# Batch 0's routing moved into the linear attention's last two blocks, with a second query buffer in the last block

## The reference, cut to what matters

```python
def _L1_attn_ref(x, Wq, Wk, Wv, Wo, bo):          # 32 heads of 64
    q, k, v = relu(proj(Wq)), relu(proj(Wk)), proj(Wv)
    kv = einsum('bhsd,bhse->bhde', k, v)
    normalizer = clip(einsum('bhsd,bhd->bhs', q, k.sum(axis=2)), 1e-06, None)
    out = einsum('bhsd,bhde->bhse', q, kv) / normalizer[..., None]
    return out @ Wo + bo
...
def _L1_ffn_ref(x, ...):                          # 64 experts, 6 of them per token, 32 slots each
    scores = softmax(x @ gate_w.T); topk_w, topk_i = top_k(scores, 6)
    # the first 32 tokens that chose an expert fill its slots; SwiGLU per expert; weighted sum
    shared = silu(x @ sw_gate) * (x @ sw_up) @ sw_down
    return y + shared
x = _layernorm(x + _L1_attn_ref(x, ...))
x = _layernorm(x + _L1_ffn_ref(x, ...))
```

## Time and profile before

| | before |
|---|---|
| median of three runs (lowest to highest) | 1489.11 us (1487.36 to 1490.24) |
| the profiled execution's own time | 1489.89 us |
| its span in the profile | 1488.1 us |
| PE busy / DVE busy / ACT busy / POOL busy | 1402.1 / 934.1 / 577.7 / 555.8 us |
| chain that ended last, PE / DVE / POOL / ACT / DMA | 81% / 7% / 4% / 2% / 2% |
| PE busy in the 40 slices, last ten digits | 9999788990 |
| PE clock granted, last ten digits | 9999899986 |

### The profile page before, as it was taken

One profiled execution on the slowest core, in us unless ns is written; L12 is line 12 of the kernel. 1 busy time (PEld: TensorE's weight loads), 2 busy tenths in 40 slices (PEclk: granted clock), 3 DMA queues, 4 the chain that ended last, 5 costly groups with the idle time before them and its releaser, 6 DMA issues.

```text
span 1488.1 us, 23868 instructions
## 1 busy us (share of the span) xinstructions
PE 1402.1 (94%) x8118; PEld 1119.1 (75%) x8118; DVE 934.1 (63%) x2158; ACT 577.7 (39%) x1457; POOL 555.8 (37%) x483
## 2 busy tenths in 40 slices
PE   9999999999999999899999999999999999788990
PEld 7777777777777777677777688788788788665650
DVE  5777777777777777773443466565665665676113
ACT  4444444444444444542122243343343333342322
POOL 3655555555555555300014122523523522204223
PEclk9999999999999999999999999999999999899986
DMA  5000000000002000110000110200200001957984
GB/s 180 1 11 1 12 0 11 0 11 0 11 0 65 8 0 0 21 65 0 1 0 1 41 39 15 72 8 16 71 7 14 8 8 44 272 179 224 279 230 127
DMA packets 68221, 76.39 MB, mean 51 GB/s; under 512 B 14205, under 2 KB 55445, under 8 KB 68149
## 3 DMA queue, kind: packets, MB, share of 16 engines
q1 hardware_dynamic: 56517, 58.36, 13.6%
q10 hardware_dynamic: 8560, 12.36, 2.7%
q0 software_dynamic: 3072, 4.72, 1.6%
HBM read 66.22 MB, written 9.21 MB: 51 GB/s over the span
## 4 chain that ended last, share of the span: by engine, by line
PE 81%; DVE 7%; POOL 4%; ACT 2%; issue 2%; DMA 2%; SPq 1%; POOLq 0%; ACTq 0%; DVEq 0%
PE ps L1683 37%; PE ps L1822 9%; PE ps L1796 7%; PE ps L1784 5%; PE ps L1859 4%; PE ps L1950 4%; PE ps L1789 2%; PE ps L2164 2%; PE ps L2033 2%; PE ps L2229 1%; DMA wo<-in_L_attn_wo_dram 1%; PE ps L2023 1%; PE ps L2246 1%; PE ps L1824 1%; PE ps L1786 1%
## 5 line engine op out<-in xcount | busy, mean ns | idle before, releaser
L793 ACT ACTIVATE probs<-ps,nm 128x128 f32<-128x128 f32 (+3 forms) x256 | 134.0, 526 | 149.9 <-DVE nm L1174 149.8
L636 POOL TENSOR_TENSOR qk<-q,ksb 128x512 f32<-128x512 f32 x64 | 83.4, 1303 | 284.0 <-ACT q L888 212.2
L1822 PE MATMUL ps<-kT,qT 128*128 128x128 f32 (+3 forms) x512 | 174.5, 449 | 4.6 <-ACT probs L793 4.6
L1089 DVE TENSOR_TENSOR pT_low<-ps,pT 128x384 fp32r<-128x384 f32 (+2 forms) x256 | 99.5, 449 | 123.1 <-ACT pT L719 121.9
L1106 DVE TENSOR_TENSOR prod<-ps,rope_sb 128x1024 f32<-128x1024 f32 x128 | 149.9, 1211 | 7.3 <-PE ps L1683 7.3
L719 ACT ACTIVATE pT<-ps 128x384 fp32r<-128x384 f32 (+2 forms) x256 | 84.8, 416 | 152.6 <-PE ps L1859 152.6
L514 POOL TENSOR_TENSOR qT<-prod 64x512 f32<-64x512 f32 x64 | 81.2, 1269 | 167.5 <-DVE prod L1106 128.9
L1796 PE MATMUL ps<-U,oT 128*128 (+1 forms) x512 | 124.5, 386 | 0.0
L514 POOL TENSOR_TENSOR kT<-prod 64x512 f32<-64x512 f32 x64 | 81.4, 1272 | 108.7 <-DVE prod L1106 106.2
L1174 DVE TENSOR_REDUCE nm<-ps 128x1 f32<-128x128 f32 (+3 forms) x256 | 113.2, 481 | 9.4 <-PE ps L1824 9.4
L1231 DVE SCALAR_TENSOR_TENSOR acc<-ps,rinv,acc 128x256 f32<-128x256 f32 x256 | 109.4, 478 | 12.0 <-PE ps L1796 12.0
(11 more groups left out here) (263 smaller groups left out, 2774.0 us busy)
## 6 DMA issues: line engine op xcount, KB each, us to landing
eg<-in_L_ffn_w_gate_dram SPq DMA_DIRECT2D x16, 704.0 KB
eg<-in_L_ffn_w_up_dram SPq DMA_DIRECT2D x16, 704.0 KB
ed<-in_L_ffn_w_down_dram ACTq DMA_DIRECT2D x10, 640.0 KB
ksb<-ks_dram SPq DMA_DIRECT2D x16, 256.0 KB, 3.3
ed<-in_L_ffn_w_down_dram SPq DMA_DIRECT2D x6, 640.0 KB
rows_dram<-rows ACTq DMA_DIRECT2D x4, 640.0 KB, 3.3
acc<-in_L_attn_x_dram SPq DMA_DIRECT2D x4, 512.0 KB
wq_in<-in_L_attn_wq_dram SPq DMA_DIRECT2D x8, 256.0 KB, 2.9
```

The source lines that it names most:

```text
L636: nc.gpsimd.tensor_tensor(qk[:], q3[:], ksb[b % 2][:], ALU.mult).then_inc(qk_ready, 1)
L793: nc.scalar.activation(probs[hh][:, off:off + (i + 1) * P], ps[:, BS + i % 2, 0:(i + 1) * P], ACT.Exp, bias=nm[:, hh, i:i + 1], accum_out= ...
L1089: return nc.vector.tensor_tensor(o, whole, hi.bitcast(F32), ALU.subtract)
L1822: pe.matmul(ps[:, bank, 0:(i + 1) * P], qT[:, hh, b, i * P:(i + 1) * P], kT[:, hh, b, 0:(i + 1) * P], start=True, stop=False)
```

## The change

The diff does five things.

- **Loads.** SP loads the weights `sw_in`, `gw_in` and `swd` before the key sums of block 15, not after them. The wait in front is for the keys of block 11 and the last key weights.
- **Block 14, tile 3.** PE transposes `gw_in` (into bank 5) ahead of `grams`; ACT makes the high halves `gwT[0]` and `sw[0]`; DVE makes the rests of both and between them `rows4(0)`.
- **Block 15.** Tile 0: `turn_x3(0)` on PE behind the queries, `x3_halves(0)` on ACT, `x3_rests(0)` on DVE. Tiles 2 and 3: half of `logits(0)` each, on PE behind the outputs and ahead of `turn`.
- **Two query buffers.** In block 15 `q3` and `qk` alternate between two places, so that ACT's relu and POOL's product of tile u need only wait for the scaling of tile u - 2. DVE then runs `norms(u)` ahead of `add3`, and `scaled(u)` ahead of `turned(u - 1)`. POOL makes `countdown` between the products of tiles 61 and 62.
- **Behind block 15.** PE: `gate_up4(0, 0)`, `outputs(63)`, `turn_x3(1)`; DVE: `top_logits(0)` ahead of `turned(63)`, then `rows4(1)`, `choose(0)`, `add3(63)`, `x3_rests(1)`, the statistics of batch 3, `list_tokens(0)`; ACT: `exps4(0)`, `gate4(0, 0)`, `x3_halves(1)`, `store_rows(0)`.

The places of `x3T`, `rows`, `q3`, `qk` in SBUF are permuted so that what is written early does not lie on what is still read. The number of products, copies and bytes is the same.

```diff
         q3 = place("q3", 82, [P, CH])        # now q3s = two places (82, 44), qks = two places (84, 46)
...
-            for b in range(1, BATCH):
+            for b in range(1, BATCH - 1):
                 load_key_sums((CHUNKS - 1) * BATCH + b, b % 2)
-            sp.wait_ge(k_ready, 4 * BLOCKS)
+            sp.wait_ge(k_ready, 4 * BATCH * (CHUNKS - 1))
+            sp.wait_ge(wk3_ready, CHUNKS)
             for w, name in enumerate(("gate", "up")):
...
+            load_key_sums(BLOCKS - 1, (BATCH - 1) % 2)
...
+                        two = last and b == 3 and i > 0
-                            pool.wait_ge(norm_ready, 3 * u - 2)
-                        nc.gpsimd.tensor_tensor(qk[:], q3[:], ksb[b % 2][:], ALU.mult).then_inc(qk_ready, 1)
+                            pool.wait_ge(norm_ready, 3 * (u - 1 if two else u) - 2)
+                        at = i % 2 if last and b == 3 else 0
+                        nc.gpsimd.tensor_tensor(qks[at][:], q3s[at][:], ksb[b % 2][:], ALU.mult).then_inc(qk_ready, 1)
...
-                            act.wait_ge(qs_ready, u)
-                        relu(q3[:], ps[:, 0, :]).then_inc(q_copied, 1)
+                            act.wait_ge(qs_ready, u - 1 if two else u)
+                        relu(q3s[i % 2 if last and b == 3 else 0][:], ps[:, 0, :]).then_inc(q_copied, 1)
+                        if last and b == 3 and i == 0:
+                            x3_halves(0)
...
+                        if last and b == 3 and i:
+                            norms(u, i % 2)
                         if not (start and i < 2):
                             add3(u - 2, (b * TPB + i - 2) % TILES)
...
+                        if last and b == 3 and i:
+                            scaled(u, i % 2)
                             turned(u - 1)
...
+                        if last and b == 2 and i == 3:
+                            dve.wait_ge(sw_hi, 1)
+                            rest(gwT[1][:], ps[:, 5, 0:KD * E1]..., gwT[0][:]).then_inc(sw_lo, 1)
+                            rows4(0)
+                            dve.wait_ge(sw_hi, 2)
+                            rest(sw[1][:], sw_in[:], sw[0][:]).then_inc(sw_lo, 1)
...
+                        if i == 0 and last and b == 3:
+                            turn_x3(0)
...
+                        if i >= 2 and last and b == 3:
+                            logits(0, (2 * i - 4, 2 * i - 3))
                         if not (start and i == 0):
                             turn(u - 1)
...
-            pe.wait_ge(q_copied, BLOCKS * TPB)
-            turn_x3(0)
-            outputs(BLOCKS * TPB - 1, BLOCKS - 1, TPB - 1)
-            ... (the transposes of gw_in)
-            pe.wait_ge(added3, BLOCKS * TPB)
-            logits(0)
-            turn_x3(1)
             pe.wait_ge(sw_lo, 2)
+            pe.wait_ge(added3, BLOCKS * TPB - 1)
             gate_up4(0, 0)
+            outputs(BLOCKS * TPB - 1, BLOCKS - 1, TPB - 1)
+            pe.wait_ge(q_copied, BLOCKS * TPB)
+            turn_x3(1)
             turn_marked(0)
             logits(1)
+            pe.wait_ge(added3, BLOCKS * TPB)
             gate_up4(0, 1)
```

More of the change, by code:

```diff
@@ L317, in gate_banks, with x3_bank @@
             return (5, 6) if m != 1 else (4, 7) if b < 2 else (2, 7)
+        def x3_bank(b, k):
+            return (1, 5)[k] if b == 0 else k
         def gate_buffer(b, m):
@@ L647, in chunk3 @@
                             root16(b - 1, 8 + b)
+                        if b == 3 and i == 1 and last:
+                            pool.wait_ge(kv_ready, BLOCKS)
+                            pool.wait_ge(qk_ready, u + 1)
+                            for h in range(2):
+                                if h:
+                                    pool.wait_ge(consts4, h)
+                                iota(countdown[64 * h:64 * h + 64, :, :], [[-T, BATCH], [-1, 2 * P]], TOK - 2 * P * h)
+                            pool.wait_ge(consts4, 2)
                     if b == 1 and not last:
@@ L1464, in _ @@
             add3(BLOCKS * TPB - 2, TILES - 2)
+            top_logits(0)
             turned(BLOCKS * TPB - 1)
@@ L2056, in outputs, with turn_x3, logits @@
                 last.then_inc(out3_ready, 1)
+            def turn_x3(b):
+                pe.wait_ge(x3_ready, b * TPB + TPB)
+                wait_past(pe, x3lo_ready, b * KD)
+                for k in range(KD):
+                    if b == 0 and k == 1:
+                        pe.wait_ge(sw_lo, 1)
+                    for i in range(TPB):
+                        last = pe.transpose(ps[:, x3_bank(b, k), i * P:(i + 1) * P], rows[b % 3][:, i, k * P:(k + 1) * P], ident[:])
+                    last.then_inc(x3_turned, 1)
+            def logits(b, tiles=range(TPB)):
+                pe.wait_ge(x3lo_ready, b * KD + KD)
+                pe.wait_ge(sw_lo, 1)
+                wait_past(pe, exp4, b * TPB)
+                for i in tiles:
+                    for k in range(KD):
+                        last = mm3(ps[:, 2, i * E1:(i + 1) * E1], lambda a: x3T[b % 3][a][:, k, i * P:(i + 1) * P],
+                                   lambda c: gwT[c][:, k, :], k == 0, k == KD - 1)
+                if i == TPB - 1:
+                    last.then_inc(logits4, 1)
             def chunk3(c, first, last):
@@ L2085, in chunk3 @@
                             keys(n + 1, c_next, (b + 1) % BATCH, i + 1)
+                        if i == 3 and last and b == 2:
+                            pe.wait_ge(sw_loaded, 5 * 16)
+                            for k in range(KD):
+                                at_k = pe.transpose(ps[:, 5, k * E1:(k + 1) * E1], gw_in[:, k * P:(k + 1) * P], ident[0:E1, 0:E1])
+                            at_k.then_inc(gw_turned, 1)
                         if i == 3 and not (last and b == 3):
```

168 lines of the change are left out of this document (77 added, 91 removed).

## The result

| | before | after |
|---|---|---|
| median (lowest to highest), same chip | 1487.69 us (1487.24 to 1490.24) | 1479.72 us (1478.16 to 1483.46) |
| the profiled execution's own time | 1489.89 us | 1478.79 us |
| its span | 1488.1 us | 1477.0 us |

The ratio is 0.9939, with a 95% interval of 0.9926 to 0.9951: faster by 8 us. The profiled spans differ by 11.1 us. That is 3.1 us more than the medians have: the execution profiled before took 2.2 us more than its median, and the one after 0.9 us less.

The account below looks back on a forecast made before the run. A chain of single steps behind block 15 was taken to delay the first list, after which VectorE sets the pace. A gain of 13.4 less 2.9 us takes 10.5 off 1489.89: 1479.4, forecast 1479.2 us, range 1475.5 to 1484.5.

Parts of the forecast that it names:

- The point that I carried over: Start of the first list of tokens: 1293.5, not 1304.01, 10.5 us earlier, with the rest gaining the same.
- Steps 1 and 2: Block 14 and tile 60: early transposes make TensorE 0.3, then 1.2 us late; outputs(59) start at 1266.6.
- Step 3: Tile 61: VectorE's rests of `kvo` end at 1271.1, scaling precedes tile 60's rest, outputs(60) start at 1272.35.
- The table "takes nothing": GpSimd's list table, made 1268.0 to 1270.1 beside busy VectorE, costs nothing; 0.1 us if twice as long.
- Steps 4 and 5: Tiles 62 and 63: outputs and logits queue ahead of turns; outputs(61) at 1277.35, turn(63) at 1283.9, 2.9 us later.
- If the buffers did nothing it would be some 3 us more.: Block 15 gets about 3 us longer with two buffers; without their benefit, some 3 us more.
- What is behind the block: From turn(63) to the first list: 9.6 us instead of 23.0, a gain of 13.4.
- The table switch: Rival: ScalarE's two open table switches each take twice 1.28 us, the list 2.6 us later, 1481.8 us; chance 2%.
- `store_rows`: Slower rival: store_rows(0) blocks ScalarE, five issues at 5 us, 1494 us, deciding from about 4 us each; chance 3%.
- the falls that I feared: Rival: clock falls in the 2.6 us gap (1482 us) or ahead of outputs(62) (list 6 us later, 1485); chance 20%.
- a granted clock of half between 1281 and 1300: Sign, between block 15's end and the second list, that the prediction is wrong as a whole.
- The experts' weights: Expert loads: wait of 3.54 us grows by 0, bounds 0 and +3.5; rival: half given back, 1484.5 us, chance 5%.

Follow-up runs that it names:

- e6: Changed kernel with GpSimd's table for the lists ahead of tile 61's product, and that product behind tile 60's clip; ratio 0.9946 to the kernel before, median 1489.95 us.
- e5: Changed kernel with batch 0's logit halves moved ahead of outputs(60) and outputs(62), not ahead of turns; ratio 0.9929 to the kernel before, median 1487.08 us.
- e7: Changed kernel with the edits of e5 and e6 together; ratio 0.9929 to the kernel before, median 1487.78 us.
- e9: Changed kernel with one query buffer, VectorE's old order, and batch 0's logit halves behind turn(61) and ahead of outputs(62); ratio 0.9929 to the kernel before, median 1486.28 us.
- e1: Changed kernel with one query buffer and VectorE's old order in block 15, routing left inside it; ratio 0.9923 to the kernel before, median 1486.88 us.
- e2: Kernel before with only the two query buffers and VectorE's new order in block 15; ratio 1.0006 to the kernel before, median 1498.91 us.
- e3: Kernel before with only the router's and shared expert's weight loads and halves moved into block 14; ratio 1.0001 to the kernel before, median 1497.57 us.
- e4: Changed kernel with outputs(63) and turn_x3(1) ahead of gate_up4(0, 0) again; ratio 0.9955 to the kernel before, median 1490.66 us.

## Why the prediction was right

**The point that I carried over held.** The forecast was 1479.2 us from a list 10.5 us earlier; it was 9.65 and the median 1479.72. That the numbers lie 0.5 us apart is partly luck, twice over. In the profiles two errors cancel: the list came 0.86 us late, and behind the experts' wait the clock gave 2.15 us that I had not counted, of which the longer wait took 0.77. And in the medians I forecast a gain of 9.9 us from 1489.11, the median of three runs; five runs of the kernel before have 1487.69, and the gain is 8.0.

**Steps 1 and 2 held.** Outputs(59) start at 1266.92 (I had 1266.6); block 14 hid the halves and rows. The 0.3 us stood there ahead of every moved product: the transpose ahead of block 15's gram sums starts 0.35 us later than before (1253.12 and 1252.77).

**Step 3 failed by 0.9 us**: outputs(60) at 1273.60, not 1272.35, of which 0.3 us stood at outputs(59) already. I put the scaling and the rest behind the rests of `kvo` but took the clips ahead of them at their usual 0.17 us. With two buffers GpSimd's product of tile 61 runs beside tile 60's clip, and the table beside the next; the clips took 0.92 and 0.42 us, 1.0 us too much, and nearly all of it on VectorE's path. That is read from the ends of the rows; e6, which was to take it away, only moved it. The table "takes nothing" with bounds to 0.1 us was wrong for the same reason: I asked who waits for GpSimd, not whom GpSimd holds. Cases stood in the trace of before, where 12 of the 64 clips are drawn out: at 946.97 a clip took 1.62 us beside a GpSimd instruction of 2.39 and ended with it, at 948.59 against 948.57. I had read no row of it. The Trainium skill says in GPSIMD Engine Reference (Specifications) that GpSimd's SBUF interfaces are shared with VectorE, and in SBUF — State Buffer (Who interferes with whom) that the contention is an exclusive lock. The traces agree: both engines lose, GpSimd's product at 1272.66 took 1.41 us and not 1.29 beside a scaling.

**Steps 4 and 5 held in their increments.** From outputs(60) to turn(63) I had 11.55 us and it was 11.34. "The queue on TensorE has taken its place" is shown by e5, e7 and e9: with no logits ahead of turn(61) and turn(62), turn(63) comes up to 1.5 us earlier with two buffers, and 1.0 us with one (e9 against e1).

**One claim was wrong: "If the buffers did nothing it would be some 3 us more."** e1 has no second buffer, and turn(63) is 1.3 us earlier, not 3 later. I had priced the chain with the gap of 1.41 us that one buffer leaves as if TensorE's added work came on top of it; it went into it. e2 shows the same from the other side. So the gain of 8 us is the routing's and the tail's, and not the buffers'; how it divides between the two, no run shows.

**What is behind the block held.** From turn(63) to the list I had 9.6 us and it was 9.42. ScalarE's timeline of the kernel after:

```profile
1286.19 1.28 ACT L1002 ACT_TABLE_LOAD   x1
1287.48 0.32 ACT L1002 ACTIVATE e<-ps,nmx 128x64 f32<-128x64 f32 x1
...
1291.05 0.41 ACTq L1008 DMA_DIRECT2D rows_dram<-rows  x1
```

The table switch costs its load and no more (the next, 1288.79 to 1290.09, likewise), so that rival falls; so does `store_rows`: its issues take 0.41 to 0.84 us, where 4 us would have decided. That a long issue means a full queue, as two of the rivals had it, no run shows. Of the gain, e3 shows that the router's weights alone give nothing: the 3.78 us wait had two causes of nearly one date. e4 puts 4.6 us of the list on the tail's order and the clock together.

**The clock.** None of the falls that I feared came in the block or at logits(1); one came at 1295.38, where twelve products took 4.50 us and not 3.0, at a granted clock of 0.50 from 1295.4 to 1298.4. I had set down "a granted clock of half between 1281 and 1300" as a sign that I was wrong as a whole. It came, and it was a badly chosen sign: VectorE's lists lead there, and it cost nothing that the list of batch 1 shows (10.2 us behind the first, before and after). The slow products filled the gap of 2.6 us that I expected ahead of turn_x3(2); 0.59 us were left of it.

The argument against that rival, "no gap there is over 1.5 us", does not hold. The clock fell in block 15 in three of the ten profiles that have the routing there: behind 1.46 us in e4, 1.25 in e5 and 1.76 in e6. The same 1.46 us left it at 2.4 GHz in the kernel after and the same 1.25 us in e7. So the length of the gap alone does not tell. The price was off too: I had 6 us for a fall ahead of outputs(62), and e5 against e7 shows 1.3 us at the list.

**The experts' weights** gave back 0.8 us of the 9.65, against 0 in my sum and bounds up to 3.5: the wait is 4.40 us, not the 3.54 that I carried over.

## What to carry to other kernels

When a step is moved beside other work, ask of each engine not only who waits for it but whom it holds while it runs: a short VectorE instruction lasted until GpSimd's ended. A second buffer is worth something only if the first was what the chain waited for; test it alone before the work that fills its gaps is added. The wait of 1.41 us in the profile of before was no price for it: e2 got none of it back. And a wait that ends with one operand may have a second that ends at the same date: taking away the named one alone gave nothing.

## What the runs showed of the hardware that was not expected

- A VectorE clip of 128x8 values takes 0.17 us, and 0.25 to 1.63 us when a GpSimd instruction is running; it then ends 20 to 40 ns after it (12 of 64 clips before, 14 of 64 after). A scaling with two operands in SBUF that starts 0.10 us behind GpSimd's product takes 1.74 us, not 0.69.
- On an experiments' chip ScalarE waits 11.40 us for TensorE's first expert products while GpSimd's 16 gathers are under way, in the kernel before as in the changed one, and 0.97 us when only 4 gathers precede them; 8.09 and 4.47 us then stand beside the other 12. Holding those is worth 5.4 us there. On the first chip neither profile has such a wait. That the chip makes the difference, and nothing else in which the runs differ, is not shown.
- TensorE's clock fell towards 1.2 GHz behind a wait of 1.25 us at outputs(62) in e5 (2.68 us of products) and stayed at 2.4 GHz behind the same wait at the same place in e7 (1.70 us); behind 1.46 us it fell in e4 and stayed in the kernel after. Kernels with the same products can differ by 1.3 us at the list in this alone.
